# Attention scores from float32 keys and queries: one product a head in place of three products of split parts

## The chip, the cores and the metric

The kernel runs on one core of a Trainium2 chip. Its time is the device time of one execution, in microseconds; the number compared is the median over several executions. The core has four engines that compute: TensorE (PE in the profile; its weight loads are the rows PEld), VectorE (DVE), ScalarE (ACT) and GpSimd (POOL). SyncE (SP) starts the transfers. They run beside one another and wait for one another through semaphores.

## The reference, cut to what matters

Two layers work on x of 8 batches x 512 rows x 512 columns. The first is a feed-forward layer with a small circuit beside it and a layer norm, the second an adaptive layer norm, attention with 16 heads of 32 columns, and another feed-forward layer. The change touches the two marked lines of the second:

```python
q = (x @ Wq + bq).reshape(B, S, N_HEAD, HEAD_DIM).transpose(0, 2, 1, 3)   # marked
k = (x @ Wk + bk).reshape(B, S, N_HEAD, HEAD_DIM).transpose(0, 2, 1, 3)
v = (x @ Wv + bv).reshape(B, S, N_HEAD, HEAD_DIM).transpose(0, 2, 1, 3)
scores = jnp.einsum('bhqd,bhkd->bhqk', q / math.sqrt(HEAD_DIM), k)        # marked
scores = scores + attention_bias
scores = jnp.where(src_mask, -jnp.inf, scores.astype(jnp.float32))
probs = jax.nn.softmax(scores, axis=-1).astype(v.dtype)
ctx = jnp.einsum('bhqk,bhkd->bhqd', probs, v)
```

Everything is float32.

## The kernel before, in words

The program has three stages, one after the other: the first feed-forward layer (ffn_stage with l0 true, trace from 0 to about 795 us), the attention (attention_stage, about 795 to 1717 us) and the second feed-forward layer (to the end). Most products of 512 columns are made from split operands: a value is rounded to fp32r (a float32 form that TensorE takes in a single instruction), the remainder is kept as a second fp32r tile, and high x high, low x high and high x low are added up in PSUM. `split_product` (L288 to L290) and `part` (L1538) do that for full 128-row operands.

In the attention stage a batch is 16 blocks. Block m is head group tile = m // 4 (four heads of 32 rows, GROUP = 4) and query rows u = m % 4 (128 queries each). So there are 8 x 16 = 128 blocks. One PE block, in the order of `body` in `tensor`:

- `scores` of the next block (L1592): for the four heads of the group, queries (32 x 128) against keys (32 x 512), each head in its own 32 rows of the array and its own PSUM bank (banks 2 to 5). The key and query tile of a group lies in `nat`, 128 partitions x 4 planes x 512: QH, QL, KH, KL, the rounded and remainder parts. Three products a head, twelve matmuls a block: first all four heads of QH x KH, then of QL x KH, then of QH x KL.
- `context` of the block before (L1609): probabilities times values, plain float32, 16 calls. Four heads stand side by side in 32 columns of the array each, and four key tiles k are added up.
- four times `turn_unit` (L1621, four 128 x 128 transposes of one head's probabilities) followed by `beside`: a quarter of a projection (L1538, three of twelve split matmuls), so that a key, query, value or output tile is done in a block. KEYS, VALUES and OUTS say which block makes which. All of these accumulate in one bank, `gen` (bank 6), and `gen_free` makes PE wait until the last user of `gen` has been read.
- in block 3 of four `over` (L1579, four transposes), in blocks 5, 6 and 8 `turn_x` (L1548, four transposes of the next batch's x). Block 8 has no projection, only two `turn_x`.

ACT turns a finished projection into the rounded plane (`nat_hi_of`, L1263: read `gen`, add the bias, write fp32r), and does exponentials (L1275) and half of the copies of transposed probabilities (L1282). DVE makes the remainder plane (`nat_lo_of`, L1399: read `gen`, add the bias, subtract the rounded plane), reads the scores (L1411: add bias and mask, take the row's extremum) and makes the other copies (L1418). `gen` is free, and a key or query tile ready, when `nat_lo` has been counted up. The three inner loops run over batches 1 to 6 as a hardware loop of two batches a turn (`each_pair`).

The order of instructions is written by hand; no planner moves them.

Of the kernel before, what the change touches and what calls it, by code (L numbers as in the profile page):

```python
# [21 lines left out]
F32 = mybir.dt.float32  # L22
# [8 lines left out]
P = 128  # L31
# [262 lines left out]
KB = 1024  # L294
# [758 lines left out]
def attention_stage(nc, ctx, mem, banks, small, keep, t, scratch, ffn0, ffn1):  # L1053
# [4 lines left out]

    GROUP, BLOCKS, PHASES = 4, H // 4 * TT, H // 4
    UNITS, PHASE, SLOTS = GROUP * BLOCKS, GROUP * TT, 16  # L1060
    QH, QL, KH, KL = range(4)
    KEYS = {0: (1, 1), 4: (2, 0), 5: (2, 1), 6: (3, 0), 7: (3, 1), 10: (4, 0), 11: (4, 1), 15: (5, 0)}
    OUTS = {1: (0,), 2: (1,), 3: (2, 3)}
    VALUES = {9: 0, 12: 1, 13: 2, 14: 3}
# [11 lines left out]
              for i, n in enumerate("kqvo")}  # L1076
    xin0, xin8, xres = at(W2H, "xin0", [P, TT, D]), at(W2H + 24 * KB, "xin8", [P, TT, D]), at(XRES, "xres", [P, TT, D])
    xin = [at((W_PASS, XIN)[i] + 4 * KB, f"xin{i + 1}", [P, 2, D]) for i in range(2)]
    nat = [at(W2H + (8 + 8 * i) * KB, f"nat{i}", [P, 4, S], F32R) for i in range(2)]
    v = [at(W2H + 24 * KB, "v0", [P, KT, D]), at(ROWS, "v1", [P, KT, D])]  # L1080
    bias = at(W2L, "bias", [P, SLOTS, S])
    xth = [keep.xth, at(W2H, "xth1", [P, KT, S], F32R)]
# [17 lines left out]
    masked, score_mm, scored, exped, turned, pt_even, pt_odd, pv_mm = map(sem, (  # L1100
        "masked", "score_mm", "scored", "exped", "turned", "pt_even", "pt_odd", "pv_mm"))
    x_mm, nat_mm, v_mm, o_mm, over_mm = map(sem, ("x_mm", "nat_mm", "v_mm", "o_mm", "over_mm"))
    xt_hi, xt_lo, nat_hi, nat_lo, v_out, o_out, over_out = map(sem, (
        "xt_hi", "xt_lo", "nat_hi", "nat_lo", "v_out", "o_out", "over_out"))
    inv_set, spread_set, normed, ct_hi, ct_lo, res_ready = map(sem, (
        "inv_set", "spread_set", "normed", "ct_hi", "ct_lo", "res_ready"))
    passed_dve, passed_sp = sem("passed_dve"), sem("passed_sp")
# [141 lines left out]
    def scalar(act, f0, f1):  # L1249
# [7 lines left out]
            act.wait_ge(x_mm, x_count(b) + k + 1)  # L1257
            nc.scalar.activation(xth[odd][:, k, :], bank[:, :], ACT.Copy).then_inc(xt_hi, 1)

        def nat_hi_of(b, tile, query, bank):  # L1260
            act.wait_ge(nat_mm, nat_count(b, tile, query))
            column = (bqc if query else bkc)[:, tile:tile + 1]
            nc.scalar.activation(nat[tile % 2][:, QH if query else KH, :], bank[:, :], ACT.Identity, bias=column).then_inc(nat_hi, 1)  # L1263

        def values(b, odd, i, bank, rows_done=False):
            act.wait_ge(v_mm, b * TT + i + 1)
# [34 lines left out]

        f0["run"](beside)
        act.wait_ge(consts_in, 16 * len(consts))
        nat_hi_of(0, 0, 0, gen)
        act.wait_ge(bq_set, 1)
        nat_hi_of(0, 0, 1, ctx_ps)
        values(0, 0, 0, gen)
        for i in range(TT):
            f0["last_norm"](0, i)
# [5 lines left out]
        def body(b, odd, first, last):  # L1315
            for m in range(BLOCKS):
                phase, u = divmod(m, TT)
                if u == 0 and phase:
                    over(b, phase - 1, first)
                elif u == 0 and not first:  # L1320
                    over(b - 1, PHASES - 1)
                before = m - 1
                if before in TURNS and not last:
                    turn_hi(b + 1, 1 - odd, TURNS[before], turn[0])
                if before in KEYS:
                    tile, query = KEYS[before]
                    if tile < KT:
                        nat_hi_of(b, tile, query, gen)
                    elif not last:
                        nat_hi_of(b + 1, tile - KT, query, gen)  # L1330
                if m == 0:
                    nat_hi_of(b, 1, 0, gen)
                if before in VALUES and not last:
                    values(b + 1, 1 - odd, VALUES[before], gen, first)
                after = following(b, m, last)
                turn_out(b, m, 0, first)
                if after:
                    exp(*after, 0)
                if m == 8 and not last:
                    turn_hi(b + 1, 1 - odd, 2, gen)  # L1340
                elif m in LAST_TURNS and last:
                    turn_hi(b + 1, 1 - odd, LAST_TURNS[m], gen)
                if after:
                    exp(*after, 1)
                if u == 0 and phase:
                    context_hi(b, phase - 1, first)
                elif u == 0 and not first:
                    context_hi(b - 1, PHASES - 1)
                turn_out(b, m, 2, first)
                if after:  # L1350
                    exp(*after, 2)
                    exp(*after, 3)
                if first and m in (1, 2):
                    for k in (2 * m - 2, 2 * m - 1):
                        split(3, k)
                if first and m in (3, 4):
                    for i in (2 * m - 6, 2 * m - 5):
                        f0["last_norm"](1, i)
                if last and m in (4, 5):
                    for i in (2 * m - 8, 2 * m - 7):  # L1360
                        f1["first_norm"](i)
                if last and m in EARLY_HI:
                    for c, k in EARLY_HI[m]:
                        f1["split"](c, k)
# [6 lines left out]
    def vector(dve, f0, f1):  # L1371
# [21 lines left out]
            dve.wait_ge(xt_hi, x_count(b) + k + 1)  # L1393
            nc.vector.tensor_tensor(xtl[odd][:, k, :], bank[:, :], xth[odd][:, k, :].bitcast(F32), ALU.subtract).then_inc(xt_lo, 1)

        def nat_lo_of(b, tile, query, bank):
            dve.wait_ge(nat_hi, nat_count(b, tile, query))
            hi, lo = (QH, QL) if query else (KH, KL)
            nc.vector.scalar_tensor_tensor(nat[tile % 2][:, lo, :], bank[:, :], (bqc if query else bkc)[:, tile:tile + 1],  # L1399
                                           nat[tile % 2][:, hi, :].bitcast(F32), ALU.add, ALU.subtract).then_inc(nat_lo, 1)  # L1400

        def output(b, i, bank):
            dve.wait_ge(o_mm, b * TT + i + 1)
            dve.wait_ge(res_ready, b * TT + i + 1)
# [44 lines left out]
                    set_mask(0, u, True)  # L1449

        f0["run"](beside)
        nat_lo_of(0, 0, 0, gen)
        nat_lo_of(0, 0, 1, ctx_ps)
        f0["last_stats"](0)
        f0["last_shift"](0)
        for j in range(GROUP):
# [2 lines left out]
        def body(b, odd, first, last):  # L1459
            for m in range(BLOCKS):  # L1460
# [2 lines left out]
                before = m - 1  # L1463
                if before in TURNS and not last:
                    turn_lo(b + 1, 1 - odd, TURNS[before], turn[0])
                if before in KEYS:
                    tile, query = KEYS[before]
                    if tile < KT:
                        nat_lo_of(b, tile, query, gen)
                    elif not last:  # L1470
                        nat_lo_of(b + 1, tile - KT, query, gen)
                if m == 0:
                    nat_lo_of(b, 1, 0, gen)
                if before in OUTS and not first:
                    output(b - 1, OUTS[before][-1], gen)
                if after:
# [53 lines left out]
    def tensor(pe, f0, f1):  # L1530
# [51 lines left out]
        def scores(b, m, first=False):  # L1582

            tile, u = divmod(m, TT)
            if u == 0:
                pe.wait_ge(nat_lo, nat_count(b, tile, 1))
            if m or not first:
                pe.wait_ge(scored, b * UNITS + GROUP * m)
            for q, k in ((QH, KH), (QL, KH), (QH, KL)):
                for j in range(GROUP):  # L1590
                    head = nat[tile % 2][j * HD:(j + 1) * HD, :, :]
                    mm = pe.matmul(score[j][:, :], head[:, q, u * P:(u + 1) * P], head[:, k, :],  # L1592
                                   start=(q, k) == (QH, KH), stop=k == KL)
                    if k == KL:
                        mm.then_inc(score_mm, 1)

        def context(b, odd, m, first):

# [25 lines left out]
        def gen_free(b, m, first):  # L1624

            if m in OUTS and m - 1 in OUTS:
                pe.wait_ge(o_out, b * TT - TT + OUTS[m][0])
            elif m in OUTS or (m == 4 and first):
                pe.wait_ge(nat_lo, nat_count(b, 1, 1))
            elif m == 4:  # L1630
                pe.wait_ge(o_out, b * TT)
            elif m == 9:
                pe.wait_ge(xt_lo, x_count(b + 1) + KT)
            elif m in (10, 13, 14):
                pe.wait_ge(v_out, b * TT + TT + (1 if m == 10 else VALUES[m]))
            elif m == 12:
                pe.wait_ge(nat_lo, nat_count(b + 1, 0, 1))
            elif m == 15:
                pe.wait_ge(v_out, b * TT + 2 * TT)
            else:  # L1640
                tile, query = KEYS[m]
                pe.wait_ge(nat_lo, nat_count(b, tile, query) - 1)

        def beside(b, odd, m, j, first, last):
            some = range(3 * j, 3 * j + 3)
# [9 lines left out]
            elif m in OUTS and not first:  # L1655
                if j == 0:
                    gen_free(b, m, first)
                if len(OUTS[m]) == 1:
                    output(b - 1, OUTS[m][0], some, gen)
                elif j < 2:  # L1660
                    output(b - 1, OUTS[m][0], range(6 * j, 6 * j + 6), gen)
                elif j == 3:
                    pe.wait_ge(o_out, b * TT - TT + OUTS[m][1])
                    output(b - 1, OUTS[m][1], ALL, gen)
            elif m == 8 and j == 1 and not last:
                pe.wait_ge(nat_lo, nat_count(b, 3, 1))
                turn_x(b + 1, 2, gen)
            elif m in LAST_TURNS and j == 1 and last:
                if m == 9:
                    pe.wait_ge(nat_lo, nat_count(b, 3, 1))  # L1670
                else:
                    pe.wait_ge(xt_lo, x_count(b + 1) + LAST_TURNS[m])
                turn_x(b + 1, LAST_TURNS[m], gen, True)
# [7 lines left out]
        pe.wait_ge(w_lo, 3)  # L1681
        for i in range(TT):
            if i < 2:
                pe.wait_ge(nat_lo, i + 1)
            else:
                pe.wait_ge(v_out, i - 1)
            values(0, i, ALL, (gen, ctx_ps)[i % 2])
# [175 lines left out]
```

## Time and profile before

| | us |
|---|---|
| median of 3 executions (2432.8 to 2438.77) | 2437.83 |
| profiled execution, its own time | 2438.72 |
| its span, first to last instruction | 2436.9 |
| PE busy, share of the span | 2378.8, 98% |
| DVE busy | 1356.6, 56% |
| ACT busy | 1011.8, 42% |
| POOL busy | 1017.2, 42% |

How to read it: a matmul's recorded time runs from its start to the end of its drain, and the next one starts before that drain is over. So busy time hides short waits; distances between starts say more than durations. A row of the timeline merges neighbours of one kind: "1450.14 0.97 ... x12" are twelve matmuls, the first of which starts at 1450.14 us and the last of which ends 0.97 us later. A plain float32 call that is no transpose leaves two matmul records: the 2048 calls of `context` are 4096 records in the trace.

### The profile page before, as it was taken

What the parts mean: (1) busy time and instruction counts of PE and PEld (TensorE: products, weight loads), DVE (VectorE), ACT (ScalarE), POOL (GpSimd) and SP (SyncE); (2) the same over time, 40 slices, a digit from 0 to 9 for tenths busy, and PEclk for the clock granted to TensorE, in tenths of its full rate; (3) what the DMA queues carried; (4) which work ended last, traced back from release to release, by engine and by line L of the source; (5) the groups of instructions that cost most, each with busy time, mean ns of one, the idle gap of its engine ahead of it and who ended that gap; (6) DMA issues with size and microseconds to landing.
All of it is one profiled execution on the core that took longest, in us unless ns stands there. A gap on an engine that the chain in (4) does not pass through costs nothing. (4 is left out here: it accounts for less than half of the span.)

```text
span 2436.9 us, 44424 instructions
## 1 busy us (share of the span) xinstructions
PE 2378.8 (98%) x16068; PEld 1903.5 (78%) x16068; DVE 1356.6 (56%) x2749; ACT 1011.8 (42%) x2057; POOL 1017.2 (42%) x829
## 2 busy tenths in 40 slices
PE   8999999999999899999999999997999999999999
PEld 6788888888887677777777777776888888888887
DVE  7355454454465777776777777778443333333322
ACT  6132232232242766766666676767321211211111
POOL 0042242341334886767676676767022112202200
PEclk9999999999999999999999999998999999999999
DMA  7110110101133455565556566565320110110100
GB/s 227 44 44 18 47 55 18 43 34 43 43 96 113 148 186 183 178 198 152 192 161 197 154 193 191 172 190 178 117 82 1 52 52 0 52 52 0 52 35 18
DMA packets 141841, 244.21 MB, mean 100 GB/s; under 512 B 13756, under 2 KB 28236, under 8 KB 141664
## 3 DMA queue, kind: packets, MB, share of 16 engines
q1 hardware_dynamic: 141664, 241.92, 31.1%
q8 instruction: 103, 1.69, 0.3%
q14 instruction: 74, 0.61, 0.1%
HBM read 216.69 MB, written 25.20 MB: 99 GB/s over the span
## 5 line engine op out<-in xcount | busy, mean ns | idle before, releaser
L1219 POOL TENSOR_TENSOR at_bias<-at_bias,at_mask 128x512 f32<-128x512 f32 x512 | 593.2, 1186 | 261.9 <-DMA at_bias<-in_fside_Bx16xSxS 241.6
L645 ACT ACTIVATE L_hid<-bank,L_b1c 128x512 f32<-128x512 f32 x256 | 176.6, 690 | 964.3 <-PE bank L290 964.3
L837 DVE CAST L_hh<-L_hid 128x512 fp32r<-128x512 f32 x256 | 123.6, 483 | 747.4 <-PE bank L946 713.8
L288 PE MATMUL bank<-xth,L_w1h 128*128 128x512 f32 x1024 | 403.3, 394 | 1.4 <-DVE xtl L730 1.4
L944 PE MATMUL bank<-L_w2h,L_hh 128*128 128x512 f32 x1024 | 401.5, 392 | 0.0
L289 PE MATMUL bank<-xth,L_w1l 128*128 128x512 f32 x1024 | 399.9, 391 | 0.0
L290 PE MATMUL bank<-xtl,L_w1h 128*128 128x512 f32 x1024 | 399.6, 390 | 0.0
L946 PE MATMUL bank<-L_w2l,L_hh 128*128 128x512 f32 x1024 | 399.1, 390 | 0.0
L945 PE MATMUL bank<-L_w2h,L_hl 128*128 128x512 f32 x1024 | 398.9, 390 | 0.0
L1275 ACT ACTIVATE at_bias<-at_bias,cos_sin 128x512 f32<-128x512 f32 x512 | 363.2, 713 | 9.0 <-DVE cos_sin L1411 8.9
L1411 DVE CUSTOM_DVE_ANT_0 at_bias<-bank,at_bias 128x512 f32<-128x512 f32 x512 | 332.6, 684 | 37.1 <-PE bank L1592 25.9
L540 POOL TENSOR_TENSOR rstd<-mv,power 128x4 f32<-128x4 f32 x24 | 26.1, 1087 | 736.2 <-DVE mv L721 736.2
L1621 PE MATMUL bank<-ident,at_bias 128*128 128x128 f32 x2048 | 314.7, 279 | 14.8 <-DVE at_pt L1418 10.7
L1621 PEld LDWEIGHTS bank<-ident,at_bias 128*128 128x128 f32 x2048 | 244.2, 142 | 90.8 <-issue 33.2
L1282 ACT ACTIVATE at_pt<-bank 128x512 f32<-128x512 f32 x256 | 152.6, 596 | 250.9 <-PE bank L1621 250.7
L839 DVE TENSOR_TENSOR L_hl<-L_hid,L_hh 128x512 fp32r<-128x512 f32 x256 | 232.5, 908 | 8.8
L1418 DVE COPY at_pt<-bank 128x512 f32<-128x512 f32 x256 | 176.2, 688 | 104.9 <-PE bank L1621 104.3
L288 PEld LDWEIGHTS bank<-xth,L_w1h 128*128 128x128 f32 x1024 | 192.7, 188 | 49.8 <-issue 8.2
L290 PEld LDWEIGHTS bank<-xtl,L_w1h 128*128 128x128 f32 x1024 | 192.7, 188 | 41.0
L289 PEld LDWEIGHTS bank<-xth,L_w1l 128*128 128x128 f32 x1024 | 192.8, 188 | 39.5
L946 PEld LDWEIGHTS bank<-L_w2l,L_hh 128*128 128x128 f32 x1024 | 192.2, 188 | 40.1
L945 PEld LDWEIGHTS bank<-L_w2h,L_hl 128*128 128x128 f32 x1024 | 192.5, 188 | 39.0
(205 smaller groups left out, 3238.9 us busy)
## 6 DMA issues: line engine op xcount, KB each, us to landing
at_bias<-in_fside_Bx16xSxS SPq DMA_DIRECT2D x256, 512.0 KB, 3.7
L_ring<-in_L_cond_w SPq DMA_DIRECT2D x32, 256.0 KB, 4.5
L_xres<-in_x SPq DMA_DIRECT2D x8, 1024.0 KB, 5.3
x_scratch<-L_xres SPq DMA_DIRECT2D x8, 1024.0 KB, 4.3
at_xres<-x_scratch SPq DMA_DIRECT2D x8, 1024.0 KB, 7.4
L_xin<-x_scratch SPq DMA_DIRECT2D x8, 1024.0 KB, 5.6
L_xres<-x_scratch SPq DMA_DIRECT2D x8, 1024.0 KB, 5.6
L_xin<-in_x SPq DMA_DIRECT2D x7, 1024.0 KB, 5.3
```

Source lines behind the costliest of these rows:

```text
L288: nc_mm = pe.matmul(out, ah, bh, start=i == 0, stop=False)
L289: nc_mm = pe.matmul(out, al, bh, start=False, stop=False)
L290: nc_mm = pe.matmul(out, ah, bl, start=False, stop=i == n - 1)
L645: nc.scalar.activation(hid[m % 2][:, :], turn[m % 2][:, :], func, bias=b1c[:, m:m + 1]).then_inc(h_act, 1)
L839: nc.vector.tensor_tensor(hl[m % 2][:, :], hid[m % 2][:, :], hh[m % 2][:, :].bitcast(F32), ALU.subtract)\
L944: pe.matmul(acc[i][:, :], hh[m % 2][:, cut], w2h[:, m, :], start=m == 0, stop=False)
L945: pe.matmul(acc[i][:, :], hl[m % 2][:, cut], w2h[:, m, :], start=False, stop=False)
L946: mm = pe.matmul(acc[i][:, :], hh[m % 2][:, cut], w2l[:, m, :], start=False, stop=m == FT - 1)
L1219: nc.gpsimd.tensor_tensor(tile, tile, mask[:, m % TT, :], ALU.add).then_inc(masked, 1)
L1275: nc.scalar.activation(tile, tile, ACT.Exp, bias=neg_top[:, n % SLOTS:n % SLOTS + 1], scale=-1.0, accum_out=sums[:, n:n + 1]).then_inc(exp ...
L1411: nc.vector.tensor_tensor_reduce(bias[:, slot, :], score[j][:, :], bias[:, slot, :], -1.0, -MASKED, ALU.add, ALU.min, neg_top[:, slot:slot ...
L1621: mm = pe.transpose(turn[n % 2][:, k * P:(k + 1) * P], bias[:, n % SLOTS, k * P:(k + 1) * P], keep.ident[:, :])
```

## The change

Keys and queries are kept as plain float32 and multiplied once. `nat` gets two planes (Q, K) in float32. `nat_hi_of` becomes `nat_out_of` and writes float32 at the same point of ACT's order. `nat_lo_of` and its eight calls a batch on DVE are gone. Everything that waited for the semaphore `nat_lo` waits for `nat_out`, which ACT counts up. `scores` has four calls a block in place of twelve. The projections, whose sums feed these planes, are the same split products as before, and so are values, context and output.

```diff
-    QH, QL, KH, KL = range(4)
+    Q, K = range(2)
-    nat = [at(W2H + (8 + 8 * i) * KB, f"nat{i}", [P, 4, S], F32R) for i in range(2)]
+    nat = [at(W2H + (8 + 8 * i) * KB, f"nat{i}", [P, 2, S]) for i in range(2)]
...
-        def nat_hi_of(b, tile, query, bank):
+        def nat_out_of(b, tile, query, bank):
             act.wait_ge(nat_mm, nat_count(b, tile, query))
             column = (bqc if query else bkc)[:, tile:tile + 1]
-            nc.scalar.activation(nat[tile % 2][:, QH if query else KH, :], bank[:, :], ACT.Identity, bias=column).then_inc(nat_hi, 1)
+            nc.scalar.activation(nat[tile % 2][:, Q if query else K, :], bank[:, :], ACT.Identity, bias=column).then_inc(nat_out, 1)
...
-        def nat_lo_of(b, tile, query, bank):
-            dve.wait_ge(nat_hi, nat_count(b, tile, query))
-            hi, lo = (QH, QL) if query else (KH, KL)
-            nc.vector.scalar_tensor_tensor(nat[tile % 2][:, lo, :], bank[:, :], (bqc if query else bkc)[:, tile:tile + 1],
-                                           nat[tile % 2][:, hi, :].bitcast(F32), ALU.add, ALU.subtract).then_inc(nat_lo, 1)
...
             if u == 0:
-                pe.wait_ge(nat_lo, nat_count(b, tile, 1))
+                pe.wait_ge(nat_out, nat_count(b, tile, 1))
             if m or not first:
                 pe.wait_ge(scored, b * UNITS + GROUP * m)
-            for q, k in ((QH, KH), (QL, KH), (QH, KL)):
-                for j in range(GROUP):
-                    head = nat[tile % 2][j * HD:(j + 1) * HD, :, :]
-                    mm = pe.matmul(score[j][:, :], head[:, q, u * P:(u + 1) * P], head[:, k, :],
-                                   start=(q, k) == (QH, KH), stop=k == KL)
-                    if k == KL:
-                        mm.then_inc(score_mm, 1)
+            for j in range(GROUP):
+                head = nat[tile % 2][j * HD:(j + 1) * HD, :, :]
+                pe.matmul(score[j][:, :], head[:, Q, u * P:(u + 1) * P], head[:, K, :], start=True, stop=True).then_inc(score_mm, 1)
...
             elif m in OUTS or (m == 4 and first):
-                pe.wait_ge(nat_lo, nat_count(b, 1, 1))
+                pe.wait_ge(nat_out, nat_count(b, 1, 1))
...
                 tile, query = KEYS[m]
-                pe.wait_ge(nat_lo, nat_count(b, tile, query) - 1)
+                pe.wait_ge(nat_out, nat_count(b, tile, query) - 1)
```

PE's order at the scores of one block before (banks 2 to 5 are the four heads' score banks, bank 7 is the context's, at_nat1 the keys and queries of the odd head groups):

```order
L1592 MATMUL bank2<-at_nat1 128x512 [waits at_scored]
L1592 MATMUL bank3<-at_nat1 128x512
L1592 MATMUL bank4<-at_nat1 128x512
L1592 MATMUL bank5<-at_nat1 128x512
L1592 MATMUL bank2<-at_nat1 128x512
L1592 MATMUL bank3<-at_nat1 128x512
L1592 MATMUL bank4<-at_nat1 128x512
L1592 MATMUL bank5<-at_nat1 128x512
L1592 MATMUL bank2<-at_nat1 128x512
L1592 MATMUL bank3<-at_nat1 128x512
L1592 MATMUL bank4<-at_nat1 128x512
L1592 MATMUL bank5<-at_nat1 128x512
```

Here each head is met three times, with the three others between. The same place after the change, on the same engine, with the start of the context product behind it:

```order
L1575 MATMUL bank2<-at_nat1 128x512 [waits at_scored]
L1575 MATMUL bank3<-at_nat1 128x512
L1575 MATMUL bank4<-at_nat1 128x512
L1575 MATMUL bank5<-at_nat1 128x512
L1589 MATMUL bank7<-at_pt,at_v0 32x128 [waits at_pt_odd,at_pt_even]
```

Each head is met once, in a float32 call; what stands in front of and behind the scores has not moved.

DVE's order before, from the last copy of one block to the copy in the middle of the next (at_nat is the remainder plane, at_bias and cos_sin what the score reader writes):

```order
L1418 COPY at_pt<-bank 128x512 [waits at_turned]
L1397 ISA
L1399 SCALAR_TENSOR_TENSOR at_nat<-bank,at_biases,at_nat 128x512 [waits at_nat_hi]
L71 REGISTER_ALU
L1411 ISA at_bias,cos_sin<-bank,at_bias 128x512 [waits at_masked,at_score_mm]
L1411 ISA cos_sin 128x1
L71 REGISTER_ALU
L1411 ISA at_bias,cos_sin<-bank,at_bias 128x512 [waits at_masked,at_score_mm]
```

The same place after the change:

```order
L1412 COPY at_pt<-bank 128x512 [waits at_turned]
L71 REGISTER_ALU
L1405 ISA at_bias,cos_sin<-bank,at_bias 128x512 [waits at_masked,at_score_mm]
L1405 ISA cos_sin 128x1
L71 REGISTER_ALU
L1405 ISA at_bias,cos_sin<-bank,at_bias 128x512 [waits at_masked,at_score_mm]
```

The pass that wrote the remainder plane stood ahead of the score reader and is gone; the rest of DVE's order is the same. ACT's order has not changed.

## Rows read from the trace of the kernel before

**Rows 1.** The page: busy time of the engines.
```profile
PE 2378.8 (98%) x16068; PEld 1903.5 (78%) x16068; DVE 1356.6 (56%) x2749; ACT 1011.8 (42%) x2057; POOL 1017.2 (42%) x829
```

**Rows 2.** Stretches: attention stage, one at the low clock. PE, PEld, DVE, ACT, POOL; clock.
```profile
794.60:1700.00 905.40, 865.32 (x9209) 666.80 (x9208) 677.74 (x1570) 620.92 (x1471) 645.90 (x554) 0.97 0.58 180
...
1319.20:1322.60 3.40, 3.40 (x46) 2.23 (x44) 2.68 (x7) 1.35 (x5) 2.28 (x2) 0.50 0.92 263
```

**Rows 3.** Timeline of PE, ordinary blocks: start us, us, what, count.
```profile
1470.36 0.96 PE L1592 MATMUL bank<-at_nat 32*128 32x512 f32 x12
1471.25 1.08 PE L1609 MATMUL bank<-at_pt,at_v 128*32 128x128 f32 x32
1472.26 0.66 PE L1621 MATMUL bank<-ident,at_bias 128*128 128x128 f32 x4
...
1476.92 0.97 PE L1592 MATMUL bank<-at_nat 32*128 32x512 f32 x12
```

**Rows 4.** Waits of PE, whole span: us in total, times, longest us.
```profile
PE bank L1621 <- DVE at_pt L1418: 10.7, 13, 2.5
...
PE bank L1592 <- DVE cos_sin L1411: 5.2, 8, 1.4
...
PE bank L1538 <- DVE at_nat L1399: 2.5, 4, 1.0
```

**Rows 5.** Timeline in narrow windows, one block's scores.
```profile
1305.40 0.51 PE L1592 MATMUL bank<-at_nat 32*128 32x512 f32 x4
...
1305.74 0.63 PE L1592 MATMUL bank<-at_nat 32*128 32x512 f32 x8
...
1305.97 0.40 PE L1592 MATMUL bank<-at_nat 32*128 32x512 f32 x4
1306.30 0.32 PE L1609 MATMUL bank<-at_pt,at_v 128*32 128x128 f32 x4
```

**Rows 6.** Groups by line and shape: count, busy us, mean ns.
```profile
L1609 PE MATMUL bank<-at_pt,at_v 128*32 128x128 f32 x4096 | 146.3, 286 | 4.6 <-issue 3.4 <-DVE at_pt L1418 1.2
...
L279 PE MATMUL bank<-L_w_pass,su_emb_off 128*8 128x512 f32 x16 | 7.2, 593 | 0.0
```

**Rows 7.** Timeline of three float32 products of 512 columns, first stage.
```profile
60.90 3.60 PE L279 MATMUL bank<-L_w_pass,su_emb_off 128*8 128x512 f32 x8
...
81.44 1.09 PE L965 MATMUL bank<-L_amp_prob,circuit 16*96 16x512 f32 x2
82.47 0.60 PE L279 MATMUL bank<-L_w_pass,su_emb_off 128*8 128x512 f32 x1
```

**Rows 8.** Timeline in narrow windows, one block's context product.
```profile
1306.30 0.42 PE L1609 MATMUL bank<-at_pt,at_v 128*32 128x128 f32 x8
...
1306.43 0.51 PE L1609 MATMUL bank<-at_pt,at_v 128*32 128x128 f32 x12
```

**Rows 9.** Timeline of block 8 of one batch: ACT, DVE, PE.
```profile
1430.50 0.67 ACT L1263 ACTIVATE at_nat<-bank,at_biases 128x512 fp32r<-128x512 f32 x1
1432.47 0.60 ACT L1282 ACTIVATE at_pt<-bank 128x512 f32<-128x512 f32 x1 [1.30 <-PE bank L1621]
...
1435.46 0.59 ACT L1282 ACTIVATE at_pt<-bank 128x512 f32<-128x512 f32 x1
...
1431.20 0.75 DVE L1399 SCALAR_TENSOR_TENSOR at_nat<-bank,at_biases,at_nat 128x512 fp32r<-128x512 f32 x1 [1.43 <-ACT at_nat L1263]
1431.87 0.68 DVE L1411 CUSTOM_DVE_ANT_0 at_bias<-bank,at_bias 128x512 f32<-128x512 f32 x1
...
1434.52 0.63 PE L1621 MATMUL bank<-ident,at_bias 128*128 128x128 f32 x4 [0.74 <-DVE at_pt L1418]
1436.11 0.66 PE L1548 MATMUL bank<-ident,at_xin 128*128 128x128 f32 x4 [0.96 <-ACT at_pt L1282]
```

**Rows 10.** Timeline of PE, start of block 9 of the same batch.
```profile
1437.60 1.08 PE L1609 MATMUL bank<-at_pt,at_v 128*32 128x128 f32 x32
1438.91 0.63 PE L1621 MATMUL bank<-ident,at_bias 128*128 128x128 f32 x4 [0.23 <-DVE xtl L1394]
```

More of the change, by code:

```diff
@@ L1102, in attention_stage @@
     x_mm, nat_mm, v_mm, o_mm, over_mm = map(sem, ("x_mm", "nat_mm", "v_mm", "o_mm", "over_mm"))
-    xt_hi, xt_lo, nat_hi, nat_lo, v_out, o_out, over_out = map(sem, (
-        "xt_hi", "xt_lo", "nat_hi", "nat_lo", "v_out", "o_out", "over_out"))
+    xt_hi, xt_lo, nat_out, v_out, o_out, over_out = map(sem, (
+        "xt_hi", "xt_lo", "nat_out", "v_out", "o_out", "over_out"))
     inv_set, spread_set, normed, ct_hi, ct_lo, res_ready = map(sem, (
@@ L1303, in scalar @@
         act.wait_ge(consts_in, 16 * len(consts))
-        nat_hi_of(0, 0, 0, gen)
+        nat_out_of(0, 0, 0, gen)
         act.wait_ge(bq_set, 1)
-        nat_hi_of(0, 0, 1, ctx_ps)
+        nat_out_of(0, 0, 1, ctx_ps)
         values(0, 0, 0, gen)
@@ L1327, in body @@
                     if tile < KT:
-                        nat_hi_of(b, tile, query, gen)
+                        nat_out_of(b, tile, query, gen)
                     elif not last:
-                        nat_hi_of(b + 1, tile - KT, query, gen)
+                        nat_out_of(b + 1, tile - KT, query, gen)
                 if m == 0:
-                    nat_hi_of(b, 1, 0, gen)
+                    nat_out_of(b, 1, 0, gen)
                 if before in VALUES and not last:
@@ L1451, in vector @@
         f0["run"](beside)
-        nat_lo_of(0, 0, 0, gen)
-        nat_lo_of(0, 0, 1, ctx_ps)
         f0["last_stats"](0)
@@ L1465, in body @@
                     turn_lo(b + 1, 1 - odd, TURNS[before], turn[0])
[L1466 to L1473, printed above, removed]
                 if before in OUTS and not first:
@@ L1636, in gen_free @@
             elif m == 12:
-                pe.wait_ge(nat_lo, nat_count(b + 1, 0, 1))
+                pe.wait_ge(nat_out, nat_count(b + 1, 0, 1))
             elif m == 15:
@@ L1665, in beside @@
             elif m == 8 and j == 1 and not last:
-                pe.wait_ge(nat_lo, nat_count(b, 3, 1))
+                pe.wait_ge(nat_out, nat_count(b, 3, 1))
                 turn_x(b + 1, 2, gen)
@@ L1669, in beside @@
                 if m == 9:
-                    pe.wait_ge(nat_lo, nat_count(b, 3, 1))
+                    pe.wait_ge(nat_out, nat_count(b, 3, 1))
                 else:
@@ L1683, in tensor @@
             if i < 2:
-                pe.wait_ge(nat_lo, i + 1)
+                pe.wait_ge(nat_out, i + 1)
             else:
```

## The prediction

> **What bounds the kernel now.** I read the page first: PE is busy 98% of the span [rows 1], so the question is whether the attention stage, the only one touched, is bound by PE's own stream or by what PE waits for. The stretches answer half of it: from 794.6 to 1700 us PE is busy 865 of 905 us, DVE 678, ACT 621, POOL 646 [rows 2]. Busy time hides waits shorter than a drain, so I then took starts from the timeline. Two ordinary blocks start their scores at 1470.36 and 1476.92, 6.56 us apart [rows 3], and the blocks with one projection and no extra transposes repeat that distance. A distance so constant is the engine's own stream: nothing is waited for there. The waits view agrees: over the whole span PE waited 10.7 us for DVE's copies, 5.2 for the score reader and 2.5 for the pass that is removed [rows 4]. So each 0.1 us added to a block on PE is worth about 0.1 x 128 = 13 us at the end, and time taken from DVE is worth nearly nothing by itself.
>
> **PE: the score products before.** In one block four heads start together at 1305.40, the next four at 1305.74, the last four at 1305.97, and the context product at 1306.30 [rows 5]. So four heads in four row strips cost the time of one: a round of fp32r products takes 0.23 us (1305.74 to 1305.97), the first 0.34 (0.11 more, which I read as the weights of its successor not being there yet), and from the last round to the context it is 0.33 (0.10 more than a round). Sum 0.90; the ordinary block has 0.89 [rows 3].
>
> **PE: after.** A float32 call of 512 columns is not one instruction of 0.23 us. Where the kernel has such calls they leave two records each, as the 2048 calls of the context are 4096 [rows 6]. At L279 eight records take 3.60 us, the last one 0.59 of it [rows 6, 7], so they start (3.60 - 0.59) / 7 = 0.43 us apart: a call is 2 x 0.43 = 0.86 us, where three fp32r products are 3 x 0.23 = 0.69. That is the heart of it: one float32 product costs five quarters of the three that it replaces. Whether four strips still overlap isn't shown for this form (32 rows, float32, 512 columns). The nearest row is the context: float32, four heads in four column strips, 128 columns. There four records are running first [rows 5], then eight, and the second four have started at 1306.43, 0.13 after the first [rows 8]; all 32 take 1.08 us [rows 3], so a round of four takes (1.08 - 0.29) / 7 = 0.11 us, a quarter of 0.43 for a quarter of the columns. So float32 calls of four strips do run together, in eight rounds of four, although the two records of a call follow each other in the program. I take the same for the row strips: two rounds.
>
> New block: first round 0.43 + 0.11 = 0.54 (the extra of the fp32r rounds), second round to the context 0.43 + 0.10 = 0.53. A check from L965, float32 with 96 columns of weights: second record at 81.44 + 1.09 - 0.59 = 81.94, 0.50 after the first, and the next line at 82.47, 0.53 later [rows 7]. Sum 1.07 against 0.90 or 0.91: **+0.16 a block, x 128 = +20.5 us**. Bounds: below, both extras gone, 0.86 - 0.90 = -0.04, x 128 = -5; above, no overlap between strips, 8 x 0.43 + 0.10 + 0.11 - 0.90 = 2.75, x 128 = +352. I take the value by the context rows, since they share the type and the four-strip order, and the fp32r rows show that the row direction overlaps too.
>
> The Trainium skill speaks against this overlap ("TensorE: Matmul & The Clock Gate", "The mechanism"): matmuls start and end in strict program order, and only weight loads are pulled ahead. By that rule the context would show one or two starts a round; the trace doesn't agree, with four running and then eight.
>
> **Where the +0.16 is covered.** Only where PE waits for something that doesn't move with it. In block 8 PE waits 0.96 us at 1436.11 for ACT's copy [rows 9]. That chain starts from PE itself: ACT begins at 1432.47, when the first transposed unit is there, and works in order up to the copy that ends at 1436.05, with no idle before it; the unit comes after the scores and the context. So it moves by 0.16 too: no cover. In block 9 the transposes start 1.31 us after the context [rows 10], where an ordinary block has 1.01 [rows 3]: 0.30 of waiting for the remainder of the next batch's x, whose transposes stood ahead of the scores. That covers the 0.16, in the 7 batches that have a next: -1.1.
>
> **DVE: one pass less, eight times a batch.** 64 passes of 0.75 us [rows 9] leave, 48 us of DVE's 678. In block 8 the pass stands at 1431.20 to 1431.95 and the score reader right behind it, though by PE's times the scores were there by about 1430.8; the reader gets up to 1 us earlier. What is late next there is ACT's chain: the 0.74 us at 1434.52 shrink, and the 0.96 at 1436.11 grow by as much. Elsewhere PE's own stream comes next. What can come back is the 2.5 us of waits for this very pass (the bank is free when ACT has written, at 1431.17 in place of 1431.95), and I give 2 of the 5.2 + 10.7 us behind DVE's readers and copies, since most of the copies' part is block 8. Together -4.5; bounds 0 and all of it, -18.4.
>
> ACT's pass stays where it is and writes as many bytes; I give it its 0.67 us again: nothing. No transfer moves. PE has eight records a block for the scores in place of twelve, and its stream isn't bound by their number: nothing. The feed-forward stages are the same.
>
> **Sum:** +20.5 - 1.1 - 4.5 = +14.9 on the profiled execution's own 2438.7, so 2453.6; the median shown is 2437.8, 0.9 lower. I say **2454 us**, slower by 0.6%.
>
> **Rivals.**
> 1. Staircase (10%). The first record of a head waits behind the second of the head before it: rounds go 0a, 0b+1a, 1b+2a, 2b+3a, 3b, five in place of two. 3 x 0.43 = 1.29 more, with 0.16 it is 1.45 a block, x 128 = +186: about 2620 us. For it: the form isn't in the trace, and the first round of the context has the shortest columns. Against: rows 8. It is also what the Trainium skill's rule above gives.
> 2. The lighter DVE wins (7%): faster. The place is the boundary of blocks 8 and 9. The stage has a mean granted clock of 0.97 [rows 2], so some 0.03 x 905 x 2 = 54 us at half clock (1.2 in place of 2.4 GHz), and stretches such as that from 1319.2, at 0.50 for 3.4 us [rows 2], lie right behind the gaps of block 8. If the pass taken away closes the gaps, six such stretches give back half of their 3.4 us, -10, and PE's waits for DVE all go, -18.4: with +20.5 - 1.1 it is -9, 2430 us. It decides from the point where more than 19 us come back. Against it: ACT's chain keeps the gap open, and ordinary blocks have no wait to give.
> 3. No change that can be told (8%). The extras of 0.11 and 0.10 halve with fewer, longer rounds: 0.965 - 0.905 = 0.06, x 128 = +8, less 5.6: 2441 us. For it only that the form is new; against it L965, which has them in full.
> 4. The forecast (75%): 2446 to 2466. Of this +/-5 is for half-clock stretches that come or go, the rest for waits given back (0 to -10) and the extras.
>
> **Numbers.** About 0.3% (7 us) is what a measurement of this kernel tells from no change. Slower: the 10%, and the 75% but for a few hundredths that end under 2445, 0.84. Same: the 8% and some of both neighbours, 0.10. Faster: 0.06. The range leaves the staircase out above and the lighter DVE below: 2441 to 2474.
>
> **What would show it.** Right: two records a call at the score line (1024 in all), 0.6 us each, in two rounds of four 0.54 apart; the context 1.07 us after the scores; ordinary blocks 6.72 us in place of 6.56; DVE some 48 us less busy; block 8 longer by 0.16. Wrong: five or more rounds (rival 1), score blocks under 0.98 (rival 3), block 8 shorter and the stage's clock near 1.00 (rival 2).

## The result and the profile after

The changed kernel takes 2454.27 us (median of 4, 2447.53 to 2457.24) against 2436.71 us (median of 4) before: a ratio of 1.007, 95% interval 1.0044 to 1.0097. It is slower by 17.6 us, 0.7%. In a second comparison on one chip it had 2453.04 us (6 executions) against 2436.95 (18), ratio 1.0063 (1.0045 to 1.0081).

The page of the changed kernel, busy time of the engines:

```profile
PE 2389.2 (98%) x15556; PEld 1872.1 (77%) x15556; DVE 1310.5 (54%) x2685; ACT 1010.9 (41%) x2057; POOL 1016.3 (42%) x829
```

Against [rows 1] PE has 512 matmul records fewer and 10.4 us more busy time, DVE 64 passes and 46.1 us less, ACT and POOL are as before.

The attention stage as one stretch (length, then PE, PEld, DVE, ACT, POOL busy, granted clock):

```profile
792.70:1708.80 916.10, 876.08 (x8701) 635.74 (x8700) 634.30 (x1510) 620.68 (x1471) 643.48 (x553) 0.99 0.56 177
```

Against [rows 2] the stage is 10.7 us longer, at a mean clock of 0.99 in place of 0.97. This profiled execution is the fastest of the four (2447.53 us), and its clock over the whole span is 0.995; the other three have 0.992 to 0.993 and 2451.9 to 2457.2 us. So the profile shows less loss than the median.

PE's timeline of two ordinary blocks after:

```profile
1452.53 1.14 PE L1575 MATMUL bank<-at_nat 32*128 32x512 f32 x8
1453.60 1.08 PE L1589 MATMUL bank<-at_pt,at_v 128*32 128x128 f32 x32
...
1459.29 1.14 PE L1575 MATMUL bank<-at_nat 32*128 32x512 f32 x8
1460.37 1.08 PE L1589 MATMUL bank<-at_pt,at_v 128*32 128x128 f32 x32
```

The starts of the scores are 6.76 us apart where they were 6.56 [rows 3]; from the scores to the context it is 1.07 or 1.08 us where it was 0.89 to 0.91. Narrow windows of the second of these blocks show how:

```profile
1459.29 0.71 PE L1575 MATMUL bank<-at_nat 32*128 32x512 f32 x4
...
1459.83 0.61 PE L1575 MATMUL bank<-at_nat 32*128 32x512 f32 x4
1460.37 0.32 PE L1589 MATMUL bank<-at_pt,at_v 128*32 128x128 f32 x4
```

Two rounds of four records, the second 0.54 us after the first and the context 0.54 after the second: the four strips overlap as they did with fp32r [rows 5], and the two records of a head are in different rounds. In the trace all four of the second round, and none of the first, carry the signal that a head's scores are done. The first four end 0.71 after the first start, the second four 0.61 after theirs (a matmul's recorded end is modelled). The weight loads of the same two rounds (PEld, two narrow windows):

```profile
1459.29 0.20 PEld L1575 LDWEIGHTS bank<-at_nat 32*128 32x128 f32 x4 [0.36 <-issue]
...
1459.40 0.20 PEld L1575 LDWEIGHTS bank<-at_nat 32*128 32x128 f32 x4
```

The second round's weights are loaded by 1459.60, 0.23 us before that round starts, so it doesn't wait for them. The first round's loads begin only with the round itself. So I read the 0.1 more as the first round waiting for its own weights.

All score records, grouped, and PE's waits:

```profile
L1575 PE MATMUL bank<-at_nat 32*128 32x512 f32 x1024 | 148.7, 651 | 10.9 <-DVE cos_sin L1405 6.5 <-issue 4.4
```

```profile
PE bank L1532 <- ACT at_pt L1282: 12.6, 7, 1.8
PE bank L1601 <- DVE at_pt L1412: 7.7, 5, 1.8
PE bank L1575 <- DVE cos_sin L1405: 6.5, 8, 1.4
```

Against [rows 4] PE waits 3.0 us less for DVE's copies, not at all for the pass that is gone, and 1.3 more for the score reader; and its seven waits for ACT's copy in block 8 are 12.6 us where they were 7.1. That is the trade that block 8 was to make. The line of before for that copy:

```profile
PE bank L1548 <- ACT at_pt L1282: 7.1, 7, 1.1
```

The distances between score starts give one number a block. These are medians over the eight batches, taken from the timelines of the profiled executions, with the comparisons' ratios. An ordinary block is one of 1, 2, 10, 14; the columns 8 and 9 are those blocks, the stage clock is the mean granted clock of the attention stage. Block 9 often holds a stretch at the low clock, so its median says little of waits:

| kernel | ordinary | 8 | 9 | stage clock | ratio to before (95%) |
|---|---|---|---|---|---|
| before | 6.57 | 6.91 | 8.00 | 0.97 | |
| after | 6.76 | 7.07 | 7.49 | 0.99 | 1.0063 (1.0045 to 1.0081) |
| DVE pass kept | 6.76 | 7.08 | 6.93 | 0.99 | 1.0086 (1.0072 to 1.0100) |
| fp32r products, no DVE pass | 6.57 | 6.90 | 7.65 | 0.98 | 0.9963 (0.9950 to 0.9976) |
| head by head | 6.59 | 6.93 | 7.97 | 0.98 | 1.0000 (0.9989 to 1.0011) |
| two fp32r products | 6.35 | 6.67 | 6.92 | 0.99 | 0.9945 (0.9925 to 0.9965) |
| float32, half the keys | 6.33 | 6.65 | 6.93 | 0.98 | 0.9931 (0.9914 to 0.9947) |
| before, copy first | 6.59 | 6.40 | 7.35 | 0.99 | 1.0009 (1.0000 to 1.0019) |
| after, copy first | 6.77 | 6.47 | 7.47 | 0.99 | 1.0065 (1.0048 to 1.0083) |
| before, x a block earlier | 6.57 | 6.35 | 8.12 | 0.98 | 1.0003 (0.9992 to 1.0014) |
| after, x a block earlier | 6.77 | 6.02 | 7.09 | 0.99 | 1.0047 (1.0031 to 1.0063) |

The low clock hides part of what these kernels do. Each execution has its mean granted clock on record. A stretch of PE at 0.50 does half of its work, so length x (1 - granted clock) is an estimate of what an execution lost to the low clock. It is a good one as long as PE's own stream is the limit. Taken off, it leaves what the execution would take at the full clock. Means over the executions, beside the kernel before in the same comparison:

| kernel | lost to the low clock, us (before) | rest, against before, us |
|---|---|---|
| after | 17.6 (21.1) | +18.9 |
| DVE pass kept | 16.7 (21.1) | +25.5 |
| fp32r products, no DVE pass | 18.4 (21.1) | -5.1 |
| head by head | 19.0 (19.3) | 0.0 |
| two fp32r products | 17.6 (19.3) | -14.3 |
| float32, half the keys | 23.6 (19.3) | -23.0 |
| before, copy first | 11.5 (21.1) | +11.8 |
| after, copy first | 12.3 (19.3) | +21.2 |
| before, x a block earlier | 18.1 (18.2) | +0.9 |
| after, x a block earlier | 11.8 (18.2) | +18.0 |

The granted clock is on record to 0.001, which is 2.4 us of one execution. The standard error of a mean is 0.6 to 2.3 us for the loss and 0.4 to 1.2 for the rest, so differences of 1 or 2 us tell nothing.

### The profile page after: what moved, and what is told of

Its sections match the earlier page's. It is cut to its first block and busy times, and to the rows that moved or that the text cites. A ratio compares the mean times of both kernels' runs of the same rounds, so it can differ in the third digit from the quotient of the medians.

```text
span 2445.7 us, 43288 instructions
## 1 busy us (share of the span) xinstructions
PE 2389.2 (98%) x15556; PEld 1872.1 (77%) x15556; DVE 1310.5 (54%) x2685; ACT 1010.9 (41%) x2057; POOL 1016.3 (42%) x829
## 5 line engine op out<-in xcount | busy, mean ns | idle before, releaser
L944 PEld LDWEIGHTS bank<-L_w2h,L_hh 128*128 128x128 f32 x1024 | 192.4, 188 | 38.9
```

Source lines behind the costliest of these rows:

```text
L944: pe.matmul(acc[i][:, :], hh[m % 2][:, cut], w2h[:, m, :], start=m == 0, stop=False)
```

## The experiments

**The changed kernel again.**

> The changed kernel unaltered, for more executions beside the three below. Main theory (PE's own stream pays 0.18 us a block, a few us come back from waits and half-clock stretches): 12 to 20 us over the kernel before. Rival (the first comparison was luck of half-clock stretches): under 8 us.

Measured: 2453.04 us, 16.1 us over the kernel before. Its ordinary blocks have 6.76 us, the stage 917.7 us. The first comparison stands.

**DVE's pass kept, for nothing.** To the changed kernel:

```diff
-    nat = [at(W2H + (8 + 8 * i) * KB, f"nat{i}", [P, 2, S]) for i in range(2)]
+    nat = [at(W2H + (8 + 8 * i) * KB, f"nat{i}", [P, 4, S]) for i in range(2)]
...
+        def nat_lo_of(b, tile, query, bank):
+            dve.wait_ge(nat_out, nat_count(b, tile, query))
+            nc.vector.scalar_tensor_tensor(nat[tile % 2][:, 2 + (Q if query else K), :], bank[:, :], (bqc if query else bkc)[:, tile:tile + 1],
+                                           nat[tile % 2][:, Q if query else K, :], ALU.add, ALU.subtract).then_inc(nat_lo, 1)
...
-                pe.wait_ge(nat_out, nat_count(b, tile, 1))
+                pe.wait_ge(nat_lo, nat_count(b, tile, 1))
```

> The changed kernel, but DVE's pass of 0.75 us a key or query tile is kept: it writes a plane that nobody reads, and PE waits for it as before. Main theory: the pass is worth its few waits, so this is 2 to 6 us slower than the changed kernel, 20 us over the kernel before; ordinary blocks stay at 6.75 us. Rival (the lighter DVE gives back much, also through the clock): 10 us or more slower than the changed kernel.

Measured: 2458.40 us, 21.5 over the kernel before and 5.4 over the changed kernel in the same comparison. The ordinary block is 6.76 us with the pass and without it. So the products alone cost about 21 us, and DVE's relief gives back about 5; the intervals of the two ratios overlap, and the 5.4 is a best value, not a bound. At the full clock it is clearer: the products cost 25.5 us, the relief gives back 6.6.

**The products kept, DVE's pass gone.** To the kernel before (L1592 and DVE's calls of nat_lo_of):

```diff
-                    mm = pe.matmul(score[j][:, :], head[:, q, u * P:(u + 1) * P], head[:, k, :],
+                    mm = pe.matmul(score[j][:, :], head[:, QH, u * P:(u + 1) * P], head[:, KH, :],
...
-                pe.wait_ge(nat_lo, nat_count(b, tile, 1))
+                pe.wait_ge(nat_hi, nat_count(b, tile, 1))
```

> The kernel before without DVE's pass: twelve fp32r products a block as before, but all of the rounded planes (the remainders are left out of the scores), and PE waits for ACT's pass. Main theory: 2 to 6 us faster than the kernel before, 2432 us; ordinary blocks 6.57 us. Rival (lighter DVE wins): 15 us faster or more, block 8 shorter by over 0.5 us.

Measured: 2427.89 us, 9.1 less than before (5.8 to 12.2 by the interval), between the two theories in size. The ordinary block is 6.57 and block 8 is 6.90, as before: no stream got shorter. With the experiment above there are two ways to the changed kernel: relief and then products, -9.1 + 25.2; products and then relief, +21.5 - 5.4. Both add up to the measured 16.1 by construction; what they tell is that each part depends on the other by about 4 us.

Four of its seven executions took 2426.5 to 2427.9 us and three 2434.1 to 2434.7. The profiled one is among the three and holds a wait of 7.18 us that the kernel before doesn't have (last section). That the other two hold it too isn't shown.

Where the relief comes back can be read from the blocks. With each block's length multiplied by its granted clock, the six inner batches (1 to 6 of 0 to 7) take 672.9 us in the kernel before and 673.1 without the pass; in the float32 kernels it is 691.7 with the pass and 691.0 without. So there the pass costs next to nothing, with either form of product, and the float32 products cost 0.19 to 0.20 us a block. It is in the first and the last batch that PE waited for the pass (four waits, 2.5 us [rows 4]). Without it blocks 0 and 5 of the first batch are shorter by 0.78 and 0.51 us, blocks 5, 6 and 8 of the last by 0.79, 0.79 and 0.74.

**The twelve fp32r products head by head.** To the kernel before:

```diff
-            for q, k in ((QH, KH), (QL, KH), (QH, KL)):
-                for j in range(GROUP):
+            for j in range(GROUP):
+                for q, k in ((QH, KH), (QL, KH), (QH, KL)):
```

> The kernel before with the same twelve fp32r products a block in another order: the three of head 0, then the three of head 1, and so on. Theory A (each row strip has its own queue and overtakes freely): three rounds as before, no change, 2437 us. Theory B (strict program order of starts): nine rounds in place of three, 6 x 0.23 x 128 = +177 us. Theory C (a strip can hold two products, the one running and the one with its weights loaded, and a third blocks what follows): each head starts a round after the one before, six rounds, 3 x 0.23 to 0.34 x 128 = +88 to +130 us. By C a float32 call, with its two records, just fits.

Measured: 2436.99 us against 2437.24, ratio 1.0000. PE's program order is now (order of this kernel):

```order
L1592 MATMUL bank2<-at_nat0 128x512 x3
L1592 MATMUL bank3<-at_nat0 128x512 x3
L1592 MATMUL bank4<-at_nat0 128x512 x3
L1592 MATMUL bank5<-at_nat0 128x512 x3
```

and the timeline in narrow windows, around the first, the second and the third start of four:

```profile
1469.70 0.53 PE L1592 MATMUL bank<-at_nat 32*128 32x512 f32 x4
...
1469.70 0.76 PE L1592 MATMUL bank<-at_nat 32*128 32x512 f32 x8
...
1470.04 0.64 PE L1592 MATMUL bank<-at_nat 32*128 32x512 f32 x8
```

Four records run, then eight have started, the second four at 1470.04, 0.34 after the first as in [rows 5]. All four of the last round, and none of the eight before, carry the signal that a head's scores are done. Head 3's first product stands behind all three of heads 0, 1 and 2 in the program, and starts with head 0's first. So a strip whose next product has to wait doesn't hold back the other strips: theory A holds, B and C fall.

**Two fp32r products.** To the kernel before:

```diff
-            for q, k in ((QH, KH), (QL, KH), (QH, KL)):
+            for q, k in ((QH, KH), (QH, KL)):
```

> The kernel before with eight fp32r products a block in place of twelve (the product of the queries' remainder is left out of the scores). Main theory (PE's own stream bounds the stage, a round costs 0.23 us): 0.23 x 120 to 128 = 28 to 30 us faster, 2408 us. Rival (waits take its place): under 15 us faster.

Measured: 2421.09 us, 16.1 less. The ordinary block fell by the full 0.22 us, so the stream bounds it and a round costs what the rows said; but the whole gave 16 in place of 28. The waits say why:

```profile
PE bank L1621 <- DVE at_pt L1418: 13.4, 12, 2.3
PE bank L1609 <- issue: 12.4, 21, 2.1
```

Both are larger than before (10.7, and 3.4 in 6 waits; L1609 is the context product, and "issue" means that the profile shows nothing it waited for). Block 13 grew from 6.63 to 6.98 us, and blocks 1, 6 and 7, with 6.52, 6.87 and 6.94, lost only 0.05, 0.16 and 0.06. I read this as DVE, which still makes its pass here, falling behind the shorter stream in more blocks. The next experiment speaks for it: its ordinary block is as short (6.33), DVE has no pass there, and its blocks 1, 6, 7 and 13 have 6.36, 6.75, 6.78 and 6.53 us. No run changes the pass alone at that length. The profiled execution is the fastest of the four (2415.78 us), so it shows less loss than the median. My main theory was half wrong: the price of a round is right, but only some of the blocks can take it as a gain. A longer stream is different: it is paid in every block.

**Half of the keys.** To the changed kernel:

```diff
-                pe.matmul(score[j][:, :], head[:, Q, u * P:(u + 1) * P], head[:, K, :], start=True, stop=True).then_inc(score_mm, 1)
+                pe.matmul(score[j][:, 0:S // 2], head[:, Q, u * P:(u + 1) * P], head[:, K, 0:S // 2], start=True, stop=True).then_inc(score_mm, 1)
```

> The changed kernel with 256 of the 512 key columns multiplied (the scores of the other half are left out). Main theory: two rounds of 0.43 become two of 0.215, the extra of 0.11 for the first weights and 0.10 for leaving stay, so a score block is 0.65 in place of 1.08: 0.43 x 128 = 55 us faster than the changed kernel, 2398 us. Rival (part of the extra grows with the columns): a score block under 0.60 us, over 62 us faster.

Measured: 2419.97 us, 33 less than the changed kernel in place of 55. The block itself is as forecast:

```profile
1456.93 0.71 PE L1575 MATMUL bank<-at_nat 32*128 32x256 f32 x8
1457.58 1.08 PE L1589 MATMUL bank<-at_pt,at_v 128*32 128x128 f32 x32
```

0.65 us for the scores, 6.33 a block, 0.43 less. So a score block is 2 x 0.43 us by its columns and 0.22 fixed (1.08 - 0.86; 0.65 - 0.43). Half of it falls before the second round and half before the context. Of the 22 us that are missing in the total, about 8 are the low clock: at the full clock this kernel is 42 us faster than the changed kernel. Another part is one wait of 8.0 us in block 11 of the first batch (last section). The profiled execution, the fastest of the four, has it; whether the others had it isn't known. The rest I put down to waits: those for "issue" at the context product, 4.8 us in the changed kernel, are 9.2 here.

**ACT's copy first in block 8.** To the kernel before, and the same to the changed kernel:

```diff
+                turn_out(b, m, 2, first)
                 if u == 0 and phase:
                     context_hi(b, phase - 1, first)
                 elif u == 0 and not first:
                     context_hi(b - 1, PHASES - 1)
-                turn_out(b, m, 2, first)
```

> The kernel before, with one swap in ACT's order in the first block of a head group: the copy of the third transposed unit ahead of the pass that writes the rounded context. Main theory (block 8 is ended by ACT's chain, as its wait of 0.96 us for that copy says): block 8 falls from 6.9 to about 6.3 us in 7 batches, 4 us, up to 10 with the half-clock stretches behind it: 2427 to 2433 us. Rival (block 8 is bound by DVE): no change.

Measured: 2440.27 us against 2436.95: no gain, if anything a loss (1.0000 to 1.0019). At the full clock it is a loss of about 12 us, and some 10 us less at the low clock hide it.

> The changed kernel with the same swap in ACT's order as in the kernel before. Main theory (ACT's chain ends block 8, and DVE's relief was hidden behind it): block 8 falls from 7.07 us by 0.6, at least as much as in the kernel before: 4 to 10 us faster than the changed kernel. Rival (DVE bound): no change.

Measured: ratio 1.0065 to the kernel before, as the changed kernel has without the swap. In both, block 8 fell by what was forecast, 6.91 to 6.40 and 7.07 to 6.47, so ACT's chain did end it. But in the kernel before, blocks 1 and 13 grew, 6.57 to 6.92 and 6.63 to 7.54. The swap delays the rounded context by a copy, DVE makes the remainder context and its own copy that much later, and the next context product waits longer. PE's waits in the kernel before with the swap, where L1609 had 3.4 us in 6 times:

```profile
PE bank L1609 <- issue: 13.5, 22, 1.5
```

With DVE's pass gone blocks 1 and 13 grew to 6.88 and 6.91 only. And block 9 kept its own chain, 7.35 and 7.47. The forecast of the place was right, that of the total was wrong: I had priced one block.

**The next batch's x a block earlier.** To the kernel before, and the same to the changed kernel (turn_x in block 8 then makes part 3):

```diff
-    TURNS, LAST_TURNS = {5: 0, 6: 1, 8: 3}, {9: 0, 10: 1, 11: 2, 12: 3}
+    TURNS, LAST_TURNS = {4: 0, 5: 1, 6: 2}, {9: 0, 10: 1, 11: 2, 12: 3}
...
-                turn_x(b + 1, 2, gen)
+                turn_x(b + 1, 3, gen)
```

> The kernel before with the next batch's x transposed one block earlier: blocks 4, 5 and 6 take a turn_x each and block 8 only one, in place of 5, 6 and two in 8. Main theory (blocks 8 and 9 are held by the chain turn_x, ACT, DVE, and every other block by PE's stream): block 4 grows by 0.43 us, block 8 falls from 6.9 to 6.0 to 6.4 and block 9 from 6.9 to 8.1 down to 6.6, in 7 batches: 4 to 12 us faster, about 2429 us. Rival (the x transfer lands too late for block 4): block 4 over 7.5 us, no gain or slower.

> The changed kernel (float32 scores) with the same move of x's transposes. Main theory: the gain adds to the change, 4 to 12 us faster than the changed kernel, 2444 us, and still 14 to 20 us slower than the kernel before with the move: the price of the float32 products is PE's own stream and isn't touched. Rival (part of the 17 us was waits at blocks 8 and 9): within 10 us of the kernel before with the move.

Measured: 2437.34 us against 2435.94 (no change), and for the changed kernel 2446.86, a ratio of 1.0047 where it has 1.0063 without the move: perhaps 4 us, the intervals overlap. Block 4 grew by 0.43 in both, as forecast. Block 8 fell to 6.35 with DVE's pass and to 6.02 without it; block 9 is 8.12 and 7.09, and didn't fall to 6.6 as forecast. So with ACT's chain cut short, DVE is late next in the kernel before and not in the changed one: here the relief that block 8 hid becomes visible, 0.33 us in 7 batches, 2 to 3 us. The two kernels with the move are 9.5 us apart, less than the 14 to 20 expected and within the 10 of the rival. But the rival's reason, waits at blocks 8 and 9, doesn't hold for most of it: at the full clock the two are 17 us apart, and the second lost 6 us less to the low clock, which makes most of the difference. The 8.12 holds low clock too: three of those seven blocks have 6.98 to 7.01. No version tried is measurably faster than the kernel before while computing all that it computes.

## Why the prediction was right

The forecast was 2454 us and 0.6% slower; measured were 2454.27 and 0.7%. That the two agree within 1 us is luck: the sum as written, +14.9 on the median of 2437.8, gives 2452.7, and two terms below are off in opposite directions.

- **PE's stream bounds the stage.** Shown: the ordinary block grew with the score block (6.56 to 6.76) and shrank with it by the full 0.22 and 0.43 us in the two experiments that shorten it.
- **Two rounds of float32 records.** Shown by the narrow windows after, and by the head-by-head order, where strips pass each other freely. Rival 1, the staircase, has fallen. The Trainium skill's rule of strict start order ("TensorE: Matmul & The Clock Gate", "The mechanism") does not hold between strips here.
- **+0.16 a block, +20.5 us.** The right mechanism, a little small: the score block is 1.08 us where I had 1.07, against 0.89 to 0.91 before, and the ordinary block grew by 0.19 where the sum had 0.16. In all 128 blocks that would be 24 us, and at the full clock the products do cost 25.5 with DVE's pass kept. The measured 21.5 is less because that kernel lost some 4 us less to the low clock (16.7 against 21.1, by an estimate with a standard error of 1.7), which the sum had at nothing (its "+/-5" for such stretches covers it). Why it loses less isn't shown.
- **The reading of the 0.11.** Right in size, wrong in its reason for float32. I put it down to the successor's weights; after the change these are there 0.23 us before their round starts. That the first round waits for its own weights fits the rows, but no experiment singles it out. In the kernel before, the rows don't decide: there the second loads end about 0.04 us before their round. The number comes out the same, since it is paid once a block either way.
- **Cover in block 9, -1.1.** Shown: where the clock stayed up, block 9 has 6.87 or 6.88 us before (two batches) and 6.82 to 6.88 after (three), so it didn't pay.
- **No cover in block 8.** Shown: 6.91 to 7.07, +0.16, with the wait for ACT's copy grown from 7.1 to 12.6 us, as the 0.74 to DVE gave way.
- **DVE's relief, -4.5.** The right size beside the float32 products (-5.4), too small beside the fp32r ones (-9.1). The bounds of 0 and -18.4 hold both. The 2.5 us of waits for this very pass did go, in the first and last batch.
- **Rival 2, the lighter DVE.** It doesn't win. The stage's mean clock did go from 0.97 to 0.99, but the kernel with the pass kept has 0.99 too, so the pass isn't shown to be the cause. By the estimate above the relief is mostly time at the full clock: -6.6 of it with float32 (the loss to the low clock is 1 us larger), -5.1 with fp32r, the three longer executions included (the loss is 3 us smaller, hardly more than its noise).

## What to carry to other kernels

A full float32 product was not the cheap way out of splitting here: at 512 columns it took 0.86 us of a strip's stream where three fp32r products took 0.69, so by these numbers dropping the split can pay only where the engine that makes the remainders is the bound. Read an engine's bound from the distance between starts of a repeated block: where it was constant, each added 0.1 us was paid every time, while each removed 0.1 us was paid out only in blocks where no other engine was just behind. Look at the first and the last turn of a loop by themselves: nearly all of the waits that one pass less on DVE removed lay there. And take the low clock out before reading a small difference: it moved by up to 10 us between kernels here, as much as most of the effects. A reorder that shortens one block has to be priced in the blocks after it too.

## What the runs showed that I had not expected

**A DVE copy can wait out a whole run of GpSimd.** DVE's copy at L1421 (the inverse sums spread over 512 columns, SBUF to SBUF) takes 0.43 us at its shortest and mostly 0.4 to 1.5. In the kernel with half the keys, in the first batch, it stands like this beside POOL's rows (timeline, DVE and POOL):

```profile
872.57 10.18 DVE L1421 COPY at_normal<-angle 128x512 f32<-128x512 f32 x1
...
870.78 5.03 POOL L1236 TENSOR_TENSOR at_xres<-at_xres,at_bor 128x512 f32<-128x512 f32 x4
...
875.76 6.71 POOL L1219 TENSOR_TENSOR at_bias<-at_bias,at_mask 128x512 f32<-128x512 f32 x6
```

POOL works without a pause from 870.78 to 882.47, and the copy ends 0.28 us after it. In the fp32r kernel without DVE's pass the same copy took 9.29 us, and ended 0.28 us after POOL's run there too (883.53):

```profile
874.52 9.29 DVE L1421 COPY at_normal<-angle 128x512 f32<-128x512 f32 x1
```

and PE waited behind it:

```profile
884.55 1.09 PE L1605 MATMUL bank<-ident,at_bias 128*128 128x128 f32 x4 [7.18 <-DVE at_pt L1412]
```

The Trainium skill ("SBUF — State Buffer", "SBUF: two separate sides") says that such a copy and a GpSimd instruction exclude each other for a whole instruction each. Most rows are in line with it: the copy is done within 1.51 us, less than one POOL instruction of 1.17 us and its own 0.43. These two are eight and nine POOL instructions long, which the rule doesn't tell. It came once in an execution, in 2 of the 12 profiles, and I made no experiment on it; that the port is the cause is argued from the two ends coinciding, not shown.

**Strips pass each other freely.** Three products deep, a waiting strip held nobody up (1.0000, 0.9989 to 1.0011). Of the two orders tried, neither is faster here.
